# Attention input stage: a halved first tile, sums of two chunks for the ones-matmuls, and another order of the statistics and norms

## The reference

```python
xn = _layernorm(x)                                   # over the features
qkv = xn @ Wqkv + bqkv ;  q, k, v = split(qkv, 3)
q = q / norm(q) ;  k = k / norm(k)
kv = sum(k * v, over the tokens)
attn = (q * kv) @ Wout + bout
h = silu(xn @ w1.T * s1) * (xn @ w2.T * s2)
h = gelu(h @ h1.T * s) ;  h = gelu(h @ h2.T * s) ;  ffn = h @ w3.T * s
out = x + attn + ffn
```

## Time and profile before

| | |
|---|---|
| median of 3 runs | 2692.21 us (2691.99 to 2804.69) |
| the profiled execution | 2691.44 us |
| its span, slowest core | 2689.5 us |
| spans of the 8 cores | 2687.2 to 2689.5 us |
| granted TensorE clock, by core | 0.992 to 0.998 |
| PE busy | 2590.6 us, 96% of the span, 11872 matmuls |
| DVE, ACT, POOL busy | 1051.2, 500.4, 211.5 us |
| HBM read | 455.20 MB |

### The profile page before, as it was taken

The page is one execution under the profiler, slowest core; times in us unless marked ns, Lnnn a source line. Parts: engine busy times, 40 slices in busy tenths (PEclk is TensorE's granted clock), DMA queues, the critical chain, the costliest instruction groups (busy, mean ns, idle before and its releaser), DMA issues.

```text
span 2689.5 us, 31255 instructions; the slowest of 8 cores (2687.2 to 2689.5 us)
## 1 busy us (share of the span) xinstructions
PE 2590.6 (96%) x11872; PEld 1161.3 (43%) x11872; DVE 1051.2 (39%) x1125; ACT 500.4 (19%) x581; POOL 211.5 (8%) x404
## 2 busy tenths in 40 slices
PE   2899999999999999999999999999999999999999
PEld 0333444444444444444444444444444444444444
DVE  2366703343333333533333532233333353333364
ACT  1455552111111111111111001111111111111110
POOL 0000000000000000000000000000000000000000
PEclk9999999999999999999999999999999999999999
DMA  7355434478555555554455974434554555545474
GB/s 166 82 122 110 87 63 94 79 133 178 121 92 88 90 84 86 87 95 84 83 91 88 199 140 77 78 63 79 87 91 82 86 87 94 85 83 91 87 138 113
DMA packets 76752, 266.39 MB, mean 99 GB/s; under 512 B 8640, under 2 KB 8768, under 8 KB 76352
## 3 DMA queue, kind: packets, MB, share of 16 engines
q0 software_dynamic: 57600, 209.74, 46.8%
q1 hardware_dynamic: 19008, 54.65, 7.1%
HBM read 455.20 MB, written 18.87 MB: 176 GB/s over the span
## 4 chain that ended last, share of the span: by engine, by line
PE 94%; DVE 2%; DMA 1%; ACT 1%; issue 1%; SPq 0%; DVEq 0%; ACTq 0%
PE ps L500 64%; PE ps L465 16%; PE ps L441 10%; PE ps L483 2%; DMA blk<-x_fm 1%; PE ps L409 1%; DVE blk L735 1%; ACT blk L564 1%; ACT blk L583 0%; DVE blk L691 0%; DVE blk L689 0%; PE ps L423 0%; SPq L339 0%; DVE tb L809 0%; ACT blk L590 0%
## 5 line engine op out<-in xcount | busy, mean ns | idle before, releaser
L500 PE MATMUL ps<-blk,ring 128*128 128x512 f16 x8064 | 1743.6, 379 | 9.2 <-DVE blk L774 2.5
L500 PEld LDWEIGHTS ps<-blk,ring 128*128 128x128 f16 x8064 | 789.0, 98 | 963.8 <-issue 15.7
L465 PE MATMUL ps<-blk,ring 128*128 128x512 f16 x2048 | 443.5, 379 | 2.0 <-DVE blk L774 1.0
L441 PE MATMUL ps<-blk,ring 128*128 128x512 f16 x1280 | 290.8, 385 | 27.4 <-DVE blk L691 20.8
L465 PEld LDWEIGHTS ps<-blk,ring 128*128 128x128 f16 x2048 | 200.3, 98 | 244.1 <-issue 2.9
L319 POOL DMA_DIRECT2D ring<-h_t x256 | 135.2, 528 | 1459.0 <-PE ps L500 1239.2
L852 DVE TENSOR_TENSOR tb<-ps,ta 128x512 f32<-128x512 f32 x72 | 49.8, 691 | 410.3 <-PE ps L500 410.3
L441 PEld LDWEIGHTS ps<-blk,ring 128*128 128x128 f16 x1280 | 125.4, 99 | 187.5 <-issue 41.7
L861 DVE TENSOR_TENSOR ring<-ring 128x2048 f16<-128x2048 f16 x72 | 88.2, 1225 | 183.3 <-PE ps L500 183.3
L619 ACT ACTIVATE blk<-ps,cst 128x512 f16<-128x512 f32 x64 | 44.0, 688 | 549.5 <-PE ps L500 549.5
L809 DVE TENSOR_TENSOR tb<-ps,tb 128x512 f32<-128x512 f32 x72 | 49.8, 692 | 190.7 <-PE ps L500 190.7
(11 more groups left out here) (45 smaller groups left out, 889.3 us busy)
## 6 DMA issues: line engine op xcount, KB each, us to landing
ring<-h_t POOLq DMA_DIRECT2D x256, 512.0 KB, 5.6
ring<-w_t POOLq DMA_DIRECT2D x96, 512.0 KB, 5.9
blk<-x_fm SPq DMA_DIRECT2D x48, 512.0 KB, 9.6
ring<-wqkv_t POOLq DMA_DIRECT2D x40, 512.0 KB, 5.5
part_fm<-blk SPq DMA_DIRECT2D x16, 512.0 KB, 10.3
blk<-part_fm SPq DMA_DIRECT2D x32, 256.0 KB, 13.0
out_fm<-blk SPq DMA_DIRECT2D x32, 256.0 KB, 7.8
ring<-wout_t POOLq DMA_DIRECT2D x8, 512.0 KB, 8.5
```

The source lines that it names most:

```text
L441: m = pe.matmul(wide(p, h), w[:, kc * 256 + jo * 128:kc * 256 + (jo + 1) * 128], rows(xn, kc)[:, h * 512:(h + 1) * 512], start=(kc == 0), ...
L465: m = pe.matmul(wide(p, h), w[:, kc * 256 + jo * 128:kc * 256 + (jo + 1) * 128], rows(xn, kc)[:, h * 512:(h + 1) * 512], start=(kc == 0), ...
L500: m = pe.matmul(bank(k, G), w[:, kc * 128:(kc + 1) * 128], chunk(OPERAND[layer][k], kc), start=(first and kc == 0), stop=(kc == 15), skip_ ...
```

## The change

- Tile 0 is cut into two pieces of 512 tokens; the other tiles are one piece each, so there are five pieces p (PIECES), and tile 0's outputs use one PSUM bank each. Its x comes in loads of two half chunks. POOL's first weight load waits for the second x pair, its third for the third x pair of the second piece.
- `stat_pair`: DVE adds two x chunks (fp32) into one bf16 buffer; ACT squares the two chunks from fp32 into sq and sq_odd, and DVE adds these; PE multiplies the two sums with the ones. `norm_pair` does the same with the squares of two output tiles of k or q (kp has four buffers, kp_odd one, `NORMS` is their order).
- PE runs the statistics of piece p + 1 in pairs behind every second output tile of k of piece p; ACT squares one x chunk behind each take of k. k's norm matmuls lie behind the first four tiles of q or v (in piece 0 the last four of v), q's behind those of v.
- `first_tiles` computes the first four k tiles of piece 0 together, chunk by chunk.
- DVE's rstd and normalise do for a piece what they did for a tile. DVE runs the key_value of tile p - 2 in the k loop of piece p, and normalises after it.

```diff
@@ -21,6 +21,11 @@
 TILES = [2, 3, 0, 1]
+PIECES = [(0, 0, 512), (0, 512, 512), (1, 0, 1024), (2, 0, 1024), (3, 0, 1024)]
+QP = (3, 4)
+NORMS = [("k", 0), ("k", 1), ("k", 2), ("k", 3), ("q", 3), ("k", 4), ("q", 4)]
...
+    def stats(p):
+        half = (p,) if p < 2 else (0, 1)
+        use(("sum", p, 0), *[2 + h for h in half])
+        use(("ssq", p, 0), *[4 + h for h in half])
+    stats(0)
+    for p, (_, lo, n) in enumerate(PIECES):
+        half = (p,) if p < 2 else (0, 1)
         for oc in range(DC):
-            use(("k", i, oc), "DC"[oc % 2])
-        use(("kn", i, 0), "A")
-        if i < 3:
-            use(("sum", i + 1, 0), "B")
-            use(("ssq", i + 1, 0), "C")
-        if i >= 2:
-            for oc in range(DC):
-                use(("q", i, oc), "DBC"[oc % 3])
-            use(("qn", i, 0), "A")
+            if p < 2:
+                use(("k", p, oc), (6, 7, 0, 1)[oc % 4])
+            else:
+                use(("k", p, oc), *pair((3, 0)[oc % 2]))
+            if p < 4 and oc == (3 if p == 0 else 1):
+                stats(p + 1)
+        use(("kn", p, 0), *[4 + h for h in half])
...
+        sq_odd = [block(6, 4096 + j * 1024, 1024).bitcast(BF16) for j in range(2)]
+        kp = [block(6, 6144 + j * 1024, 1024).bitcast(BF16) for j in range(2)]
+        kp += [ta[:, :].bitcast(BF16), tb[:, :].bitcast(BF16)]
+        kp_odd = tu[:, :].bitcast(BF16)
...
+                if pos == 0:
+                    po.wait_ge(s_x[11], 16)
+                if pos == 2:
+                    po.wait_ge(s_x[4], 16)
...
+            sp.dma_start(out=ones_sb[:, :], in_=ones_h).then_inc(s_one, 16)
+            for p in range(2):
+                if p == 1:
+                    sp.dma_start(out=cst[:, :], in_=consts).then_inc(s_ini, 16)
+                    sp.wait_ge(s_x[12], 16)
+                t0 = TILES[0] * TT + p * 512
+                for c in range(0, DC, 2):
+                    sp.dma_start(out=blk[:, c * 2048:(c + 2) * 2048].bitcast(F32).rearrange("p (c t) -> p c t", c=2)
+                                 [:, :, p * 512:(p + 1) * 512],
+                                 in_=x_hbm[c * 128:(c + 2) * 128, t0:t0 + 512].rearrange("(c p) t -> p c t", c=2)
+                                 ).then_inc(s_x[X_FILL[(p, c)][0]], 16)
+            for p in range(2, 5):
+                i = PIECES[p][0]
+                for c in range(DC):
+                    n = i * DC + c
+                    if n >= 10:
+                        sp.wait_ge(s_xn, n - 9 + DC)
+                    sp.dma_start(out=xs[n % 10], in_=x_hbm[c * 128:(c + 1) * 128, TILES[i] * TT:(TILES[i] + 1) * TT]
+                                 ).then_inc(s_x[n % 10], 16)
...
+            def stat_pair(p, j):
+                J = p * 4 + j
+                if j == 0:
+                    room(("sum", p, 0))
+                    room(("ssq", p, 0))
+                pe.wait_ge(s_xb, J + 1)
+                for out, src in zip(halves(("sum", p, 0)), steps(xb[J % 2], p)):
+                    m = pe.matmul(out, ones_sb[:, :], src, start=(j == 0), stop=(j == 3))
+                m.then_inc(s_sum, 1)
+                pe.wait_ge(s_sqp, J + 1)
+                for out, src in zip(halves(("ssq", p, 0)), steps(sq[J % 2], p)):
+                    m = pe.matmul(out, ones_sb[:, :], src, start=(j == 0), stop=(j == 3))
+                m.then_inc(s_ssq, 1)
+            def norm_pair(kind, p, j):
+                key = (kind + "n", p, 0)
+                if j == 0:
+                    room(key)
+                J = NORMS.index((kind, p)) * 4 + j
+                pe.wait_ge(s_kp, J + 1)
+                for out, src in zip(halves(key), steps(kp[j], p)):
+                    m = pe.matmul(out, ones_sb[:, :], src, start=(j == 0), stop=(j == 3))
                 m.then_inc(s_nrm, 1)
+            def out_tile(kind, p, oc):
+                i = PIECES[p][0]
+                w = landed(pe, (kind, i, oc // 2))
+                room((kind, p, oc))
+                for kc in range(DC):
+                    if oc == 0 and kind == "k":
+                        pe.wait_ge(s_xn, p * DC + kc + 1)
+                    lo = kc * 256 + oc % 2 * 128
+                    for out, src in zip(halves((kind, p, oc)), steps(rows(xn_buf[i % 2], kc), p)):
+                        m = pe.matmul(out, w[:, lo:lo + 128], src, start=(kc == 0), stop=(kc == DC - 1))
+                m.then_inc(s_mm[kind], 1)
+            def first_tiles():
+                for oc in range(4):
+                    room(("k", 0, oc))
+                w = [landed(pe, ("k", 0, oc // 2)) for oc in range(4)]
+                for kc in range(DC):
+                    if kc in (3, 5, 7):
+                        stat_pair(1, kc // 2 - 1)
+                    pe.wait_ge(s_xn, kc + 1)
+                    for oc in range(4):
+                        lo = kc * 256 + oc % 2 * 128
+                        m = pe.matmul(halves(("k", 0, oc))[0], w[oc][:, lo:lo + 128],
+                                      steps(rows(xn_buf[0], kc), 0)[0], start=(kc == 0), stop=(kc == DC - 1))
+                        if kc == DC - 1:
+                            m.then_inc(s_mm["k"], 1)
...
+            pe.wait_ge(s_one, 16)
+            for j in range(4):
+                stat_pair(0, j)
+            first_tiles()
+            stat_pair(1, 3)
+            for oc in range(4, DC):
+                out_tile("k", 0, oc)
+            for oc in range(DC):
+                out_tile("v", 0, oc)
+                if oc >= 4:
+                    norm_pair("k", 0, oc - 4)
+            for p in range(1, 5):
+                for oc in range(DC):
+                    out_tile("k", p, oc)
+                    if p < 4 and oc % 2:
+                        stat_pair(p + 1, oc // 2)
+                normed = "k"
+                if p in QP:
+                    for oc in range(DC):
+                        out_tile("q", p, oc)
+                        if oc < 4:
+                            norm_pair("k", p, oc)
+                    normed = "q"
+                for oc in range(DC):
+                    out_tile("v", p, oc)
+                    if oc < 4:
+                        norm_pair(normed, p, oc)
...
+            def square_x(p, c):
+                J = p * 4 + c // 2
+                src = x_landed(ac, p, c)
+                if c % 2 == 0 and J >= 2:
+                    ac.wait_ge(s_ssq, J - 1)
+                out = sq_odd[J % 2] if c % 2 else sq[J % 2]
+                ac.activation(seg(out, p), src, AF.Square).then_inc(s_sqx, 1)
...
+            def take(kind, p, oc):
+                i = PIECES[p][0]
+                dst, bias0, value = {"k": (kbuf, BK, p * DC + oc + 1), "v": (vbuf, BV, p * DC + oc + 1),
+                                     "q": (qbuf[i - 2], 0, (p - 3) * DC + oc + 1)}[kind]
+                dst = seg(rows(dst, oc), p)
+                if kind != "q" and i > 0:
+                    ac.wait_ge(s_tp, (i - 1) * DC + oc + 1)
+                ac.wait_ge(s_mm[kind], value)
+                ac.activation(dst, area((kind, p, oc)), AF.Identity,
+                              bias=cst[:, bias0 + oc:bias0 + oc + 1]).then_inc(s_take[kind], 1)
+                if kind == "v":
+                    return
+                n, j = NORMS.index((kind, p)), oc // 2
+                if oc % 2 == 0 and n > 0:
+                    ac.wait_ge(s_nrm, n * 4 + j - 3)
+                if oc % 2 and n * 4 + j > 0:
+                    ac.wait_ge(s_kp, n * 4 + j)
+                ac.wait_ge(s_take[kind], value)
+                ac.activation(seg(kp_odd if oc % 2 else kp[j], p), dst, AF.Square).then_inc(s_sqk, 1)
...
+            for c in range(DC):
+                square_x(0, c)
+            rstd(0)
+            for c in range(DC):
+                square_x(1, c)
+            ac.wait_ge(s_ini, 16)
+            for oc in range(DC):
+                if oc == 3:
+                    rstd(1)
+                take("k", 0, oc)
+            for oc in range(DC):
+                take("v", 0, oc)
+            inverse_norm("k", 0)
+            for p in range(1, 5):
+                for oc in range(DC):
+                    take("k", p, oc)
+                    if p < 4:
+                        square_x(p + 1, oc)
+                if p < 4:
+                    rstd(p + 1)
+                normed = "k"
+                if p in QP:
+                    for oc in range(DC):
+                        take("q", p, oc)
+                        if oc == 4:
+                            inverse_norm("k", p)
+                    normed = "q"
+                for oc in range(DC):
+                    take("v", p, oc)
+                    if oc == 4:
+                        inverse_norm(normed, p)
...
+            def stat_pair(p, j):
+                J = p * 4 + j
+                a = x_landed(ve, p, 2 * j)
+                b = x_landed(ve, p, 2 * j + 1)
+                if J >= 2:
+                    ve.wait_ge(s_sum, J - 1)
```

(100 more changed lines are left out.)

194 lines of the change are left out of this document (88 added, 106 removed).

## The result

The changed kernel takes 2669.0 us (median of 4 runs, 2668.1 to 2669.9) against 2692.1; the ratio is 0.9914, 95% interval 0.9895 to 0.9934. 2668 was forecast. The profiled execution took 2669.9 us, its slowest core (core 1) 2668.3. In several executions of the experiments some cores were granted a lower clock; where such cores set the time (e4, e6, e7), the spans of the cores with the highest granted clock are given instead of a time, and a kernel's time is 1.4 to 2 us above its longest span.

What follows compares the result with a forecast made beforehand. PE was taken as the bound, carrying 94% of the chain. Up to hidden1, 394 us at full rate plus 15 for the clock made 409 against 432.5, 23.5 less: forecast 2668 us, range 2645 to 2693.

Steps and rivals of the forecast that it cites:

- sum of 23.5 us: Total gain forecast up to hidden1's start: 409 us with the clock's cost, against 432.5 before.
- Ones-matmuls: On PE, sums of two chunks and half pieces leave 112 of 224 ones-matmuls; 24 us of work goes.
- Start: Smaller first x piece, loaded ahead of weights: last pair at 13.5 us, first normalised chunk 21.4, first_tiles and last pair end 36.0.
- The stops: In k of pieces 1 to 3, PE idles before each pair's ssq matmul: 4.0 us, four times a tile.
- Piece 0: Rest of piece 0: takes 4 to 7 queue behind kp_odd, v's first tile at 48.1; end 62.8, 5 us lost.
- The clock: Lower clock after PE's stops: 1.2 us for each of 8 stops, 3 in piece 1, 2.4 before piece 2; 15 us.
- k of piece 1: Four pairs with ACT setting the period; k ends at 97.2 us at full clock, plus 3 us for the clock.
- period of a pair at full clock: In k of piece 1, ACT's two rounds of take, square and square_x, then DVE: 8.6 us per pair.
- Ahead of piece 2: PE waits for DVE's normalisation before piece 2's first tile, some 9 us, plus 2.4 us for the clock.
- Rival 4: In k, squares of x run ahead of takes, so 12 stops and their clock vanish: 60 us less, 2608; 6%.

Runs made afterwards that it cites:

- e4: Changed kernel with 16 zero-weight matmuls added at the start of each stat_pair of pieces 2 to 4; spans 2647 to 2654 us.
- e6: Changed kernel without POOL's two waits for x, so all nine weight loads share the engines with x from the start; spans 2681 to 2689 us.
- e7: Changed kernel with the four norm_pairs of k (pieces 1 to 4) and of q together ahead of the next kind's first tile; spans 2677 to 2686 us.
- e8: Changed kernel with a zero-weight matmul added ahead of each of the 48 norm matmuls of k and q; 2678.3 us.
- e5: Kernel before the change, with POOL's first weight load waiting for the eighth x chunk of tile 0; 2663.9 us.
- e1: Changed kernel with ACT squaring each x chunk of the next piece ahead of k's take instead of behind it; 2627.5 us.
- e9: Changed kernel with PE's stat_pair one k tile later, except the last, ACT and DVE unchanged; 2630.2 us.
- e2: e1 with DVE's norm_pair of k one pair later, the last behind rstd; 2617.2 to 2619.9 us.

## Why the prediction was right

The sum of 23.5 us came out at 23.1, and the mechanism is the one named. That it came out to half a us is in part luck: the clock cost more than was summed and the work at full clock less. Step by step, forecast against core 1, the slowest:

| | forecast | measured |
|---|---|---|
| fourth x pair used | 13.5 | 13.0 |
| first product | 21.4 | 23.3, the weights came last |
| first_tiles and last pair | 36.0 | 37.5 |
| end of piece 0 | 62.8 | 65.7 |
| end of k, piece 1 | 97.2 | 100.5 |
| end of k, piece 2, at full clock | 169.8 | 178.6 |
| end of k, piece 3, at full clock | 247.4 | 261.4 |
| hidden1, with the clock | 409 | 408.1 |

**Ones-matmuls**: right, 112 fewer; e8 shows their price on the path. They are 24 us of work, but the stops of 45 us stand against them, so the gain is the start's: the first product comes 38 us earlier (61.35 before), hidden1 24.

**Start**: right in size. It was put down to a first piece of half the size whose loads go ahead of the weights, and e5 and e6 divide it: the wait on POOL moves x, with or without halves. Too optimistic was that the first two weight tiles are there when the first chunk is normalised; on core 1 that was 20.6, and they landed at 23.3. first_tiles and the pairs took 14.3 us from there, 14.6 forecast, although its first products ran at half rate: PE has time to spare between DVE's chunks.

**The stops**: right, 3.81 us in pieces 2 and 3 for 4.0 (2.76 the first, behind DVE's key_values), 3.3 to 3.5 in piece 1. e1 removes them by ACT's order, e9 most of them by PE's.

**Piece 0**: k's tiles did wait for ACT behind kp_odd, v's first tile began at 49.1 for 48.1.

**The clock** was mis-sized, and another term hid it. I took 1.2 us for each of eight stops; on core 1 all eight paid, 1.7 us each but for one of 1.4 (8.60 for 32 products instead of 6.9), 13.2 us for 9.6. For this core the rule of the Trainium skill ("TensorE: Matmul & The Clock Gate", HAM oscillation) that recurring gaps make each next batch start cold was the better guide. On other cores it held for most batches and not for all. Core 0, piece 2, the last line being where the 32 products have ended:

```profile
147.51 0.59 PE L488 MATMUL ps<-blk,ones_sb 128*128 128x512 bf16 x2 [3.81 <-DVE blk L804]
147.94 7.07 PE L511 MATMUL ps<-blk,ring 128*128 128x512 f16 x32
155.07 0.59 PE L484 MATMUL ps<-blk,ones_sb 128*128 128x512 bf16 x2
```

In k of piece 1 I had added 3 us, and 3.2 were paid: 35.0 us, against 31.8 in e4, which has no stops there. What was wrong is the period of a pair at full clock, 8.6 us in the sum and 8.0 in e4: ACT's round of take, square and `square_x` takes 2.26 us from start to start (76.95 to 79.21) and not 2.66. That is 2.6 us too much in the four pairs. Ahead of piece 2 I had added 2.4 us and none was paid, 27.9 us against 28.3 in e4, because DVE's normalisation sets the pace there. So on core 1 the clock cost 16.4 us instead of 15, and the rest came to 391.7 instead of 394.

**Rival 4**, stops absent, was false, but e1, which has just the order that this rival names, shows what it would have given: 2627, with 2608 foreseen. The rival forgot DVE, whose adds come next; with these moved too (e2) it is 2617.

## What to carry to other kernels

When work is moved between the tiles of another loop, look at what stands ahead of its producer on every queue: a consumer right behind tile n must not need anything that its producer does only after taking tile n. Move the producer ahead of the take, or the consumer one tile later; either gave 35 us or more here. And give the DMA engines first to the load that starts the chain: one wait on the queue of the later loads was worth 28 us.

## What the hardware showed unexpectedly

Whether a stop is followed by the lower clock level is not the same on every core and every time. Behind a stop of 3.8 us the next products were slow eight times in eight on core 1 (once the stop was 2.8 us), even at 220.96, where 38 us without a gap lay ahead of it, 33 of them at full rate; but on core 0 the 32 products behind two such stops, at 147.51 and 243.23, took 7.1 us. Behind the stops of piece 1 on core 1 (3.3 to 3.5 us) the 16 products took 5.1, 3.5 and 5.0 us from start to start, so there one batch of three kept the upper level. Behind stops of 0.8 us, in pieces 2 and 3 of e9, 32 products took 7.1 to 7.4 us on all eight cores. Matmuls with zero weights, whose result is nothing, kept the upper level (e4). The two bf16 adds took 0.69 us for 1024 columns and 0.42 for 512, as estimated from the 2048-column row. An x pair issued at 11.3, a microsecond behind two weight loads, was first used at 24.2, 13 us later; the four pairs of piece 0, issued from 1.5 us on with no weights beside them until 10.0, were all in use 11.5 us after the first issue.
